# A Mamba-and-attention block with experts on one core: o's statistics to ScalarE, u*D to TensorE, the scatter into the expert stage, gates with places of their own, and all places new

## What is computed

```python
x = x + _layernorm(_L0_attn_ref(_layernorm(x), ...))      # per sequence
x = x + _layernorm(_L0_ffn_ref(_layernorm(x), ...))       # over all tokens

def _mamba(x, ...):
    u, res = jnp.split(x @ in_proj_w.T, 2, axis=-1)        # 512 channels each
    u = jax.nn.silu(conv(u))                               # 4 taps
    dt, Bm, C = jnp.split(u @ x_proj_w.T, ...)             # 16 states
    delta = jax.nn.softplus(dt @ dt_proj_w.T + dt_proj_b)
    # per step t: h = exp(delta*A)*h + delta*B*u ; y = sum over states of h*C
    y = ys + u * D_skip
    return (y * jax.nn.silu(res)) @ out_proj_w.T

m = _mamba(x); h = _layernorm(m + x) ; ... q, k, mixing, h2 = _layernorm(hs + h)
o = _layernorm(gelu(h2 @ d1 + b) @ d2 + b + h2)            # the first half's output

# experts: two best of 8 per token, at most 2048 tokens each in order of tokens
out = relu(tokens @ first.T) @ second.T * weight
final = zeros.at[index].add(out)                           # dropped tokens stay 0
```

## Time and profile before

| | before |
|---|---|
| median of 3 runs | 6693.94 us |
| the profiled execution, its own time | 6735.03 us |
| its span, first to last instruction | 6733.1 us |
| VectorE / TensorE / GpSimd / ScalarE busy | 5240.0 / 5418.0 / 4435.8 / 3841.4 us |
| mean granted TensorE clock | 0.878 |
| moved by DMA | 1297.88 MB |

### The profile page before, as it was taken

One profiled execution on the slowest core, in us unless ns is written; L12 is line 12 of the kernel. 1 busy time (PEld: TensorE's weight loads), 2 busy tenths in 40 slices (PEclk: granted clock), 3 DMA queues, 4 the chain that ended last, 5 costly groups with the idle time before them and its releaser, 6 DMA issues. The chain is left out here.

```text
span 6733.1 us, 71525 instructions
## 1 busy us (share of the span) xinstructions
PE 5418.0 (80%) x16640; PEld 2989.0 (44%) x16640; DVE 5240.0 (78%) x6883; ACT 3841.4 (57%) x6622; POOL 4435.8 (66%) x2993
## 2 busy tenths in 40 slices
PE   4788888888888888888888888898888887699400
PEld 1344444444444444444444444444444444466300
DVE  4898888988898989888888888888888984111255
ACT  3566666666666666666666666666666653111255
POOL 2677777777777777777777777777777775100375
PEclk8898999998998989888998999989998987799755
DMA  7666666666665666666666666666666563122342
GB/s 254 220 222 215 218 215 214 222 217 217 217 220 208 220 217 218 214 205 205 212 211 205 211 210 210 205 211 210 206 208 215 200 207 100 50 87 87 96 145 87
DMA packets 492099, 1297.88 MB, mean 193 GB/s; under 512 B 59310, under 2 KB 216624, under 8 KB 490560
## 3 DMA queue, kind: packets, MB, share of 16 engines
q1 hardware_dynamic: 440960, 1219.82, 53.8%
q10 hardware_dynamic: 26048, 38.95, 1.7%
q0 software_dynamic: 24576, 33.72, 1.6%
HBM read 1206.19 MB, written 119.54 MB: 197 GB/s over the span
## 5 line engine op out<-in xcount | busy, mean ns | idle before, releaser
L509 POOL TENSOR_TENSOR st<-st,C_rows 128x1024 f32<-128x1024 f32 x1024 | 2486.2, 2437 | 794.0 <-DVE st L1078 790.5
L1078 DVE TENSOR_TENSOR_SCAN st<-dA,drive 128x1024 f32<-128x1024 f32 x1024 | 2339.8, 2285 | 201.5 <-ACT dA L718 67.1
L885 PE MATMUL y<-st,ident 128*128 128x512 f32 x4096 | 2138.7, 663 | 350.6 <-POOL st L509 342.4
L718 ACT ACTIVATE dA<-delta,a_neg 128x511 f32<-128x511 f32 x2048 | 1372.1, 713 | 849.4 <-DVE st L1078 723.3
L885 PEld LDWEIGHTS y<-st,ident 128*128 128x128 f32 x4096 | 832.2, 210 | 1416.6 <-issue 922.0
L1050 DVE TENSOR_TENSOR drive<-du,B_rows 128x1024 f32<-128x1024 f32 x1024 | 1259.7, 1230 | 112.3 <-DMA B_rows<-bc_rows 28.4
L1458 POOL DMA_INDIRECT rows<-expert_out,idx_c x256 | 267.3, 1044 | 626.0 <-DVE idx_c L1505 555.2
L859 PE MATMUL pre_bank<-e_abs,in_w 128*128 128x512 f32 x1024 | 565.9, 691 | 77.5 <-DVE u L1027 74.6
L838 PE MATMUL post_bank<-d_w,gT 128*128 128x256 f32 x2048 | 453.7, 380 | 27.4 <-issue 26.6
L596 POOL DMA_INDIRECT expert_in<-tb,idx x256 | 257.1, 1004 | 311.8 <-DVE idx_all L1233 235.6
L838 PEld LDWEIGHTS post_bank<-d_w,gT 128*128 128x128 f32 x2048 | 388.0, 190 | 111.6 <-issue 60.2
(11 more groups left out here) (203 smaller groups left out, 8103.6 us busy)
## 6 DMA issues: line engine op xcount, KB each, us to landing
B_rows<-bc_rows SPq DMA_DIRECT2D x1024, 512.0 KB, 3.8
C_rows<-bc_rows SPq DMA_DIRECT2D x1024, 512.0 KB, 5.2
xin<-in_x SPq DMA_DIRECT2D x32, 512.0 KB, 7.1
expert_in<-gT ACTq DMA_DIRECT2D x8, 2048.0 KB, 27.5
xn_rows<-xin SPq DMA_DIRECT2D x32, 512.0 KB, 6.2
h<-xn_rows SPq DMA_DIRECT2D x32, 512.0 KB, 7.5
x_res<-in_x SPq DMA_DIRECT2D x32, 512.0 KB, 6.4
x_rows<-x_res SPq DMA_DIRECT2D x32, 512.0 KB, 6.5
```

What stands on the lines that cost most here:

```text
L509: pool.tensor_tensor(tile[:, :, :], tile[:, :, :], bc[1][k % ROWS[1]][:, :, :], ALU.mult)\
L718: return act.activation(dA[k % 2][:, j, 1:L], delta[par][:, c, 1:L], ACT.Exp, scale=a_neg[:, c, n:n + 1])
L885: last = pe.matmul(Y[:, :], ident[:, :], st[k % RING][:, j, :], start=pair == 0 and j == 0, stop=pair == CU - 1 and j == 1)
L1078: dve.tensor_tensor_scan(st[k % RING][:, :, :].rearrange("p a l -> p (a l)"), dA[k % 2][:, :, :].rearrange("p a l -> p (a l)"), DR[:, :, : ...
```

## The change

1. *Statistics of o on ScalarE.* VectorE's bn_stats and bn_aggr of o go; ScalarE takes a sum and, after GpSimd's mean, a sum of squares (two passes of four instructions, each with an accumulator read), as it already does for the next norm.
2. *u\*D by TensorE.* One matmul with a diagonal matrix opens the sum in y for each chunk; VectorE's L1056 goes.
3. *Gates with places of their own* (30, 56, 76, and 0 of the next scan), and nearly all places of all engines are new.
4. *Scatter in the expert stage.* A token's row in the experts' input now carries its two weights, its two experts and its number (264 columns in place of 256). VectorE works out each row's weight and destination per block, multiplies by the weight while it copies from PSUM, and GpSimd writes the rows with 4 indirect DMAs per block into an array of two ranks in order of tokens. This array is zeroed in the attention phase, 1 MB per sequence.
5. *Combine without gathers.* The two ranks of a sequence come with one plain DMA of 4 KB runs, TensorE adds them with identity matmuls in PSUM, VectorE takes statistics, GpSimd makes scale and shift (power, no Ln and Exp), ScalarE normalises and issues the store, VectorE adds the first half's output, which was loaded for all sequences during the expert stage and stays in SBUF. The loop body holds 8 sequences.

```diff
+    DW = D + 8
+    xe_dram = nc.dram_tensor("expert_in", (NSLOT, DW), F32, kind="Internal").ap()
+    yr_dram = nc.dram_tensor("rank_rows", (2 * NTOK, D), F32, kind="Internal").ap()
+    yr_v = yr_dram.rearrange("(c s p t) d -> s p c t d", c=2, s=S, p=P)
...
 # SP, pre
-                at = iter((2, 26, 56, 93))
+                at = iter((0, 14, 48, 66, 95))
...
+                sp.dma_start(yr_zero_v[b].rearrange("p (a r) -> p a r", r=zeros.shape[1]), zero_row)\
+                    .then_inc(rank_rows_zeroed, 16)
...
 # GpSimd, late
-                at = iter((5, 5, 19, 25, 26, 31, 31, 43, 43, 43, 43, 43, 43, 43, 43))
+                at = iter((9, 17, 19, 24, 26, 26, 26, 32, 43, 43, 43, 43, 43, 43, 43, 47))
...
-                pool.wait_ge(*late_dve.at("o_aggr", b))
-                scale_and_shift(late_pool, "o", r_late, shift_late, mv_late, LN_EPS, b)
+                pool.wait_ge(*late_act.at("o_sum", b))
+                mean_of(late_pool, "o", shift_late, sum_late)
+                yield next(at)
+                pool.wait_ge(*late_act.at("o_sq", b))
+                scale_of(late_pool, "o", r_late, shift_late, sq_late, LN_EPS, b)
...
 # ScalarE, pre / late
-                at = iter((6, 13, 22, 22, 25, 28, 32, 33, 43, 44, 50, 51, 58, 58, 58, 58, 58, 64, 64, 67, 68, 93))
+                at = iter((10, 11, 15, 18, 19, 22, 27, 37, 40, 45, 48, 52, 52, 58, 58, 59, 59, 59, 59, 68, 69, 95))
...
-                at = iter((25, 27, 31, 36, 38, 41))
+                at = iter((21, 24, 25, 28, 33, 34, 39, 40))
+                yield next(at)
+                def junk(tile):
+                    return li[:, tile, :]
+                act.wait_ge(*late_dve.at("f_normed", b))
+                sum_of(junk, s, sum_late).then_inc(late_act.did("o_sum"), 1)
+                yield next(at)
+                act.wait_ge(*late_pool.at("o_m", b))
+                act.wait_ge(*late_act.at("o_sum", b))
+                squares_of(junk, s, shift_late, sq_late).then_inc(late_act.did("o_sq"), 1)
...
 # TensorE, scan and post
+                        pe.matmul(Y[:, :], d_diag[:, c, :], u[par][:, c, :], start=True, stop=False)
...
-                at = iter((8, 10, 26, 28, 31, 41, 49, 54, 61, 62, 74, 79, 84, 89, 93))
+                at = iter((0, 5, 23, 26, 29, 42, 49, 53, 66, 69, 74, 79, 79, 83, 92))
...
 # VectorE
-                dve.scalar_tensor_tensor(Y[:, :], u[par][:, c, :], d_skip[:, c:c + 1], Y[:, :],
-                                         ALU.mult, ALU.add).then_inc(scan_y.did(f"a{c}"), 1)
-                dve.wait_ge(*scan_y.at(f"a{c}", b))
...
+            def gates(b, par):
+                at = iter((30, 56, 76))
...
 # VectorE, late
-                at = iter((15, 18, 19, 20, 42, 42, 43))
+                at = iter((15, 17, 17, 41, 41, 43))
...
-                dve.wait_ge(*late_dve.at("f_normed", b))
-                stats(late_dve, "o", tiles_of(s), stat_late, mv_late, b)
...
 # expert phase
+                    for part in range(XL):
+                        at = (i * NB + n) * XL + part
+                        sp.dma_start(x1_all[:, bass.ds(at, 1), :, :], x1_wide_v[bass.ds(at, 1)]
...
+                    for tile in range(TB):
+                        pool.indirect_dma_start(
+                            out=yr_dram, in_=O[n % 2][:, tile, :], in_offset=None,
...
-                    for tile in range(0, TB, 2):
-                        last = dve.tensor_copy(O[n % 2][:, tile:tile + 2, :],
...
+                    for tile in range(TB):
+                        last = dve.tensor_scalar(O[n % 2][:, tile, :],
...
 # combine phase
-        G = 4
+        G = 8
+        H = 4
...
-            turns(act, ((2, normalise), (0, scaled), (1, power)))
+            turns(act, ((0, normalise), (2, store)))
...
-            turns(dve, ((4, add), (0, prepare), (2, both), (3, shifted)))
+            turns(dve, ((2, add), (0, stats)))
```

375 lines of the change are left out of this document (219 added, 156 removed).

## The result

The changed kernel takes 6398.03 us (median of 4 runs, 6392.81 to 6402.19) against 6692.72 us before in the same group of runs: ratio 0.956, 95% interval 0.954 to 0.958. Forecast were 6250 us, range 6130 to 6390: the sign is right, the time is 148 us off and 8 us outside the range. The profiled execution (6392.81 us, span 6391.0) lies at the low end of its runs.

What follows compares the result with a forecast made beforehand. VectorE was taken to bound the attention loop. From 6733.1 us of span, attention -230, start and end +6, experts +6 and combine -226 gave 6289; 6291 of execution time less 41 gave 6250 us, range 6130 to 6390.

Steps and rivals of the forecast that it cites:

- The gates' wait: Attention loop: of VectorE's 181 us waiting at the gates for TensorE's sum in y, 20 stay: -160 us.
- VectorE's work that goes: Attention loop: u*D, o's statistics and small copies leave VectorE, the bound, so all of it counts: -163 us.
- The zeroing: Attention loop: 1 MB of zeroed ranks per sequence, queued ahead of a B load: +22 us, bounds 0 and 80.
- f's statistics: Attention loop: VectorE waits 1.58 us per sequence for GpSimd between f's statistics and their use: +51 us.
- ScalarE: Attention loop: added passes and two more table loads per sequence make dA late: +20 us.
- TensorE: Attention loop: four more matmuls per sequence, 3.8 us, fill TensorE's waits for products: 0 us.
- Combine: Combine stage: without gathers, DMA or a low-clocked TensorE decides; 190 us, -226, bounds -280 (136 us) and -160 (256 us).
- The 41 us taken off at the end: Whole kernel: profiled execution stood 41 us over its runs' median, so 6291 became 6250 us.
- Rival 1: Attention loop: TensorE becomes the bound, period 172 us, total 6448 us; chance 0.12.
- Rival 2: Combine stage: stays far above DMA's time, 240 to 256 us, through TensorE at 1.2 GHz or pauses; 6300 us; chance 0.20.
- Rival 3: Loop and combine: places fit better, DMA nearer 428 GB/s; loop gains 330 us, combine takes 145, total 6105; chance 0.14.
- Rival 4: Attention loop: ScalarE holds up the scan, 17 us per sequence, total 6794 us; chance 0.05.

Runs made afterwards that it cites:

- before_gates: Kernel before with only the first three chunks' gates moved to places 30, 56 and 76: 6722.6 us against 6743.8, ratio 0.997.
- zero_tail: Changed kernel with the 32 zeroing transfers of 1 MB moved from the loop to the attention phase's end: 6362.4 us against 6398.
- scatter_pairs: Changed kernel with zeroing in the attention phase's end and GpSimd's eight scatters in pairs at places 43, 46, 49, 52: 6337.3 us.
- best_four: Changed kernel with zeroing in the phase's end, scatters two, three, three, deltas at old places, last gate at 3, x and h loads moved: 6272.4 us.
- delta_places: Changed kernel with VectorE's two deltas and the next scan's first du and drive back at places 85, 91, 94: 6349.8 us, -41 against the control.
- skip_on_dve: Changed kernel with u*D back on VectorE and TensorE's four diagonal matmuls removed: 6514.0 us, 116 to 124 more.
- before_trace: Kernel before, profiled again without edit: 6702.6 us; its combine stage took 372.8 us instead of 412.9.

## Why the prediction was right and wrong

**The gates' wait, -160: the failed step.** I wrote that the wait "should vanish there", and at the gate it did (181 to 58 us). The step that failed is counting all of it. The wait was GpSimd's lateness behind the routing seen at its first customer; the same edit alone, in the kernel before, is worth 21 us (before_gates). I worked out that the gate would be served in time and did not ask, at that same place, who else waits for GpSimd: the ring of C buffers and, through it, SP; TensorE's next matmuls and, through them, ScalarE and dA. before_gates shows the wait moving to the second pair (68 us at one unit), zero_tail, scatter_pairs and best_four show it moving between the gates, the recurrences and SP's word. No run puts the gates back in the changed kernel, so what their move is worth there is not measured.

**VectorE's work that goes, -163.** The work that goes is counted right; in time u*D, given back, costs 116 to 124 us where I had 100, and o's statistics 15 to 23 where I had 59 less 20 for ScalarE. But the term took every other instruction at its old duration, while the new places put pairs of them against GpSimd's product: +65 for delta, +24 for dv. -163 became -74. Of this, delta_places gets 41 us back in time.

**The zeroing, +22 with a bound of 80.** Waits for B rows grew by 118 us. I priced the transfer alone; at place 48 it goes out together with a C load that GpSimd held back. In time it costs 21 to 36 us, since it covers the wait above, so the term was low by 14 us at most and not by 96.

**f's statistics, +51**: 47.5 us measured, 1.58 each. **ScalarE, +20**: waits for dA fell to 19.3 us instead of rising; its lateness showed at the taps (+37.5). **TensorE, 0**: skip_on_dve speaks for it, without weighing it by itself. Start and end cost 16 us instead of 6, experts -1 instead of +6.

**Combine, -226.** The stage takes 137 us, at my lower bound of 136. DMA moved 419 GB/s in runs of 4 KB, where I took 337, the loop's rate in runs of another kind, as the nearer; and TensorE had full clock in the stage's middle (0.92 over the stage) instead of a mixture. Of the gain of 276, 40 us are the higher level of one profile, the one with the pauses: from the level of before_trace it is 236.

**The 41 us taken off at the end.** I assumed that the profile's distance from its median would stay. It sat in the stage that the change replaces, 40.1 of it in combine, and so could not be taken off again. Without this step the forecast is 6291 us.

The sum: 158 us of attention, -7 experts, -50 combine, 41 for the median, and 5 us of the new median over its own profile, make 148. The pauses, of which I expected three by the Trainium skill (Runtime: NRT & Kernel Launch, Instruction fetch mechanics), are absent in the new stage and in before_trace's, which has the same branches as the first profile. The other weighing stands undecided: by the 2.66 us per table switch of the Trainium skill (ScalarE: Activation LUTs, What ACT_TABLE_LOAD costs) the two new ones per sequence would cost 170 us in all, an estimate, and no run takes them away. The trace of the changed kernel shows no drain at them: 1.28 us each, with 0.02 us idle before and 0.01 behind (medians of 360).

**The rivals.** Rival 1 gave a period of 172 and 6448 us. The period, 170.4, is near it, its mechanism is not: TensorE is busy for 87% of the loop, not 97, and taking its new matmuls away, with u*D back on VectorE, made the loop longer. VectorE is still the busiest (4812 of 5411 us, waiting for the lock included); the waits that grew come from GpSimd being late between the routing and the second gate. Rival 2 fell. Rival 3 has the combine stage (145 us forecast) and not the loop. Rival 4 fell: dA waits are 19 us.

## What to carry to other kernels

A wait taken away is worth the distance to the next customer of the same late engine, so list all customers of that engine behind the place, not the one that waits now, and with them the engines that wait for these customers. When a queue gives word of something, see what it stands behind before blaming the thing itself. When instructions are moved, look for those whose duration depends on a neighbour: here each VectorE instruction with two SBUF inputs wants to be the first behind a recurrence, and misplaced ones show as busy time, where no table of waits finds them. If a profile is off its own median, find the stage that holds the difference before subtracting it.
